# Second cross attention of a two-layer decoder kernel: VectorE spreads the queries straight from PSUM, the keys come by DMA, GpSimd copies the context values

## The chip, the cores and the metric

The kernel runs on one core of one Trainium2 chip. The metric is the device time of one execution in microseconds (us), as the median of several runs; lower is better. The core has five engines that run their own instruction streams and meet at semaphores: TensorE (PE; PEld are its weight loads), VectorE (DVE), ScalarE (ACT), GpSimd (POOL) and SyncE (SP), which here only issues DMAs.

## What is computed

The program is two decoder layers over 128 sequences of 64 tokens with 128 features, so 8192 tokens, handled as 64 tiles of 128 tokens (two sequences each). The change touches one sub-layer, the second layer's cross attention. Its heads attend to a context of the same shape, without any projection of queries, keys or values: the normalised `x` is the query, the context is key and value, the scores are bounded by a tanh, and one output projection follows.

```python
def _L1_xattn_ref(query, key, value, mask, W_out, scale, log_C):
    B, S, E, H = (4, 256, 128, 16)
    ...
    u = jnp.einsum('hbqd,hbkd->hbqk', q, k) * scale / np.sqrt(d_k)
    logits = jnp.tanh(u) * jnp.exp(log_C)
    logits = jnp.where(mask, -jnp.inf, logits)
    attn = jax.nn.softmax(logits, axis=-1)
    out_heads = jnp.einsum('hbqk,hbkd->hbqd', attn, v)
    out = jnp.moveaxis(out_heads, 0, -2).reshape(query.shape)
    return out @ W_out.T
...
x = x + _L1_xattn_ref(_layernorm(x, axis=-1), ctx_1024, ctx_1024, mask_Bx1xS2_bk0, L1_xattn_W_out, L1_xattn_scale, L1_xattn_log_C)
```

## The kernel before

The kernel goes through ten stages one after the other (attention, output norm, cross attention, memory layer, then the second layer's attention, cross attention, routing and experts). Each stage is one software pipeline per engine, written by `staggered(nc, eng, tiles, segments)`. A segment is a pair of a lag and a function; in round s an engine works through its list in the order written and calls each function for tile s minus its lag. The engines execute in order, so an instruction that waits for a semaphore holds up all that stands behind it on its engine. `need(eng, sem, T.before(n))` and `wait_ge(sem, T.now())` are the waits; `before(2)` stands where a buffer has two copies, `before(1)` where it has one.

The stage of the change is called cross1. Per tile it does this:

- DVE `normed_rows` (line 1332) writes the normalised rows to `xn`, in SBUF.
- PE `place_q` (L1102) transposes them into the PSUM tile `psXQ`, which has one copy.
- DVE `copy_queries` (L1644) copies `psXQ` to `queries`, in SBUF.
- POOL `spread_queries` (L547) multiplies `queries` by the 0/1 constant `own_head` and writes the eight-fold wider `wide_queries`, 128x1024, in which every head has its own rows only.
- DVE `copy_ctx_keys` (L1648) copies 128 columns of the transposed context, which lies in SBUF as `cT` since the start, to `ctx_keys`. The matmul takes its weights from there.
- PE `scoresT` (L899) makes the transposed scores in `psST` (one copy). It waits for the keys (`qb_ready`), the spread queries (`kx_ready`), and the tanh of the tile before.
- ACT `tanhs` (L748) and `bounded_exps` (L752) make the probabilities in `PT`.
- SP loads a tile of the context by rows to `ctile` (L445), and DVE `ctx_values` (L1636) copies it in two halves of 64 partitions to the value block `VB`, between columns of ones.
- PE `values_of_heads` (L940) multiplies probabilities and values to `psOh`; DVE `normalised_heads` divides (L1659, L1662); PE `outputT` (L954) transposes, ACT `copy_oT` (L623) copies, PE `out_project` (L970) projects to `psXY`, DVE `add_output` (L1397) adds to `x`, and `stats_of_sum` (L1653) takes the row statistics.

The order on each engine is set by hand in the lists. The semaphores `aT_raw` and `aT_ready` say that `psXQ` is written and that it may be written again, `sT_done` that a tile's scores are done, `vb_ready` that its values are in place.

Of the kernel before, what the change touches and what calls it, by code (L numbers as in the profile page):

```python
# [7 lines left out]
P = 128  # L8
SEQ = 64
HEADS = 16  # L10
DH = P // HEADS
PAIRS = HEADS // 2
SETS = 2
PER_SET = HEADS // SETS
# [21 lines left out]
ALU = mybir.AluOpType  # L36
# [71 lines left out]
def build(nc, x, ctxT, ctx, mask, consts, rows, cols, wq0, wk0, wv0, wo0, xWq, xWk, xWvT, xWeT, wqk, keysT, key_inT,  # L108
          key_out, wq1, wk1, wv1, wo1, wout, scal, router, up, down, out):
    NT = x.shape[0] // P  # L110
    NG = NT // GROUP
    with ExitStack() as es:
# [3 lines left out]
        def sem(name):  # L116
            return es.enter_context(nc.semaphore(name))
# [9 lines left out]
        small = sb("small_w", [P, 8, P])  # L127
# [19 lines left out]
        def C(name):  # L147
            a, n = CONST[name]
            return cst[:, a:a + n]
# [40 lines left out]
        queries = KC.rearrange("p u g k -> p u (g k)")  # L190
# [155 lines left out]
        ctx_in = [sem("ctx_tile0_in"), sem("ctx_tile1_in")]  # L346
        ones_ready, sums_done, quantised, folds_done, folds_ready, bound_ready = (
# [15 lines left out]

        o_seen, xT_seen, sim_seen, ln_seen, y_seen, pe_seen = sem("o_seen"), sem("xT_seen"), sem("sim_seen"), sem("ln_seen"), sem("y_seen"), sem("pe_seen")
# [43 lines left out]
        def _(sp):  # L408
# [32 lines left out]
            ctx_v = ctx.rearrange("(t p) d -> t p d", p=P)  # L441
# [4 lines left out]
            staggered(nc, sp, NT, [(0, ctx_load)])  # L446
# [21 lines left out]
        def _(pool):  # L468
# [74 lines left out]
            def spread_queries(T):  # L543

                pool.wait_ge(aT_ready, T.now(NORM["cross1"]))
                need(pool, sT_done, T.before(2))
                pool.tensor_tensor(wide_queries[:, T.u], queries[:, T.u].unsqueeze(1).to_broadcast([P, PER_SET, P]),  # L547
                                   C("own_head").unsqueeze(2).to_broadcast([P, PER_SET, P]), ALU.mult).then_inc(kx_ready, 1)
            staggered(nc, pool, NT, [(0, spread_queries)])


# [12 lines left out]
        def _(act):  # L564
# [190 lines left out]
            staggered(nc, act, NT, [(4, copy_oT(OUTT["cross1"])), (2, tanhs), (2, bounded_exps)])  # L755
# [51 lines left out]
        def _(pe):  # L807
# [80 lines left out]
            def scoresT(base):  # L888

                def seg(T):  # L890
                    u = T.u
                    pe.wait_ge(qb_ready, T.now(base))
                    pe.wait_ge(kx_ready, T.now(base))
# [204 lines left out]
            def place_q(T):  # L1098
# [5 lines left out]
                (3, values_of_heads(b2)), (4, out_project(oT_ready, OUTT["cross1"], PROJ["cross1"], lambda u: OT[:, u, :], small[:, WOUT, :])),  # L1104
# [81 lines left out]
        def _(dve):  # L1186
# [442 lines left out]
            def ctx_values(T):  # L1629

                u = T.u
                dve.wait_ge(ctx_in[u], T.pair * 16 + 16)
                need(dve, pv_done, T.before(2, b2))
                for b in range(2):
                    part = slice(SEQ * b, SEQ * b + SEQ)
                    ins = dve.tensor_copy(VBh[part, u, :, b, 0:DH], ctile[part, u, :].rearrange("p (h d) -> p h d", h=HEADS))  # L1636
                ins.then_inc(vb_ready, 1)

            def copy_queries(T):

                u = T.u
                dve.wait_ge(aT_raw, T.now(NORM["cross1"]))
                need(dve, kx_ready, T.before(2, b2))
                dve.tensor_copy(queries[:, u, :], psXQ).then_inc(aT_ready, 1)  # L1644

            def copy_ctx_keys(T):
                need(dve, sT_done, T.before(2))
                dve.tensor_copy(ctx_keys[:, T.u, :], cTt[:, T.t, :]).then_inc(qb_ready, 1)  # L1648
# [6 lines left out]
            def normalised_heads(T):  # L1655
# [8 lines left out]
            staggered(nc, dve, NT, [(1, copy_queries), (3, ctx_values), (5, add_output("cross1", None)), (0, copy_ctx_keys),  # L1664
                                    (0, normed_rows(NORM["cross1"])), (5, stats_of_sum), (3, normalised_heads)])
# [190 lines left out]
```

## Time and profile before

| | us |
|---|---|
| median of 3 runs | 2909.44 (2908.89 to 2909.66) |
| the profiled execution, its device time | 2916.36 |
| its span from the first to the last instruction | 2914.3 |
| stage cross1, from 1856.95 to 2139.72 in the span | 282.8 |

Over the span PE is busy for 2524.5 us, DVE for 2382.4, ACT for 1835.6 and POOL for 1101.8. These are averages over stages with different limits, so the table says little on cross1 alone; the rows below are from that stage wherever their group says so. The stage runs 64 tiles.

### The profile page before, as it was taken

How to read it: one execution, taken by the hardware profiler on the slowest of the kernel's cores; microseconds unless marked ns; L12 is line 12 of the kernel's file. 1: busy time of each engine (PE TensorE's matmuls, PEld its weight loads, DVE VectorE, ACT ScalarE, POOL GpSimd, SP SyncE). 2: the span in 40 equal slices, each digit the busy share in tenths (PEclk: the TensorE clock that was granted, in tenths of full speed). 3: DMA queues.
4: the chain of work that ended last, by engine and by line, in shares of the span. 5: the costliest groups of instructions: out<-in, count | busy, mean ns of one | idle time of the engine just before them, and what ended most of it. 6: DMA issues, size and time to landing. Idle time of an engine off the chain costs nothing.

```text
span 2914.3 us, 95817 instructions
## 1 busy us (share of the span) xinstructions
PE 2524.5 (87%) x35786; PEld 1958.3 (67%) x35786; DVE 2382.4 (82%) x6431; ACT 1835.6 (63%) x3307; POOL 1101.8 (38%) x981
## 2 busy tenths in 40 slices
PE   2999963867888888888799999877789999999999
PEld 2666642546777777777566666555577888888887
DVE  6999989687899999999599999677767777777776
ACT  1777763544566666666366666565666777777776
POOL 1444420008899999999323232344413000000000
PEclk9999985977999999999799999798969999999999
DMA  5000000000000000000100000000001111111111
GB/s 165 1 0 0 0 15 0 1 0 2 1 0 0 0 0 0 0 0 0 59 1 0 0 0 0 9 15 16 14 5 52 51 55 51 54 51 54 55 53 48
DMA packets 47578, 60.44 MB, mean 21 GB/s; under 512 B 6672, under 2 KB 25872, under 8 KB 47376
## 3 DMA queue, kind: packets, MB, share of 16 engines
q1 hardware_dynamic: 47504, 59.45, 6.7%
q8 instruction: 47, 0.77, 0.1%
q14 instruction: 27, 0.22, 0.0%
HBM read 54.98 MB, written 4.46 MB: 20 GB/s over the span
## 4 chain that ended last, share of the span: by engine, by line
PE 77%; DVE 13%; issue 6%; DVEq 2%; ACT 1%; POOL 1%; DMA 0%; ACTq 0%; POOLq 0%; SPq 0%
PE ps L1064 8%; PE ps L885 8%; PE ps L1053 5%; PE ps L912 4%; PE ps L927 4%; PE ps L1078 4%; PE ps L1155 4%; PE ps L1133 4%; PE ps L1157 4%; PE ps L1156 4%; PE ps L1135 4%; PE ps L1134 4%; DVE work L1587 3%; DVE work L1636 2%; PE ps L940 2%
## 5 line engine op out<-in xcount | busy, mean ns | idle before, releaser
L479 POOL TENSOR_TENSOR work<-work,consts_sb 128x1024 f32<-128x1024 f32 x128 | 243.4, 1902 | 564.9 <-ACT work L603 564.9
L1064 PEld LDWEIGHTS ps<-work 32*32 32x32 f32 x16384 | 244.0, 145 | 126.7 <-issue 125.2
L1064 PE MATMUL ps<-work 32*32 32x32 f32 x16384 | 250.2, 226 | 76.0 <-DVE work L1587 60.8
L723 ACT ACTIVATE ps<-work 128x128 f32<-128x128 f32 x512 | 154.6, 354 | 233.6 <-DVE work L1569 222.6
L885 PE MATMUL ps<-work 128*128 128x512 f32 x512 | 262.5, 615 | 4.0 <-issue 2.8
L1730 DVE TENSOR_TENSOR h_low<-consts_sb,h_up 128x1024 fp32r<-128x1024 f32 x128 | 158.3, 1237 | 110.9 <-ACT h_up L794 110.8
L1133 PE MATMUL ps<-a_low,w_up 128*128 128x512 f32 x512 | 203.0, 396 | 0.9 <-DVE a_low L1705 0.9
L1155 PE MATMUL ps<-h_low,d_up 128*128 128x512 f32 x512 | 199.6, 390 | 2.3 <-DVE h_low L1730 2.3
L1730 DVE TENSOR_TENSOR h_low<-small_w,h_up 128x1024 fp32r<-128x1024 f32 x128 | 158.8, 1240 | 51.7 <-ACT h_up L794 51.7
L1135 PE MATMUL ps<-a_up,w_low 128*128 128x512 f32 x512 | 200.2, 391 | 0.0
L1134 PE MATMUL ps<-a_up,w_up 128*128 128x512 f32 x512 | 200.0, 391 | 0.0
L1157 PE MATMUL ps<-h_up,d_low 128*128 128x512 f32 x512 | 199.3, 389 | 0.0
L1156 PE MATMUL ps<-h_up,d_up 128*128 128x512 f32 x512 | 199.2, 389 | 0.0
L547 POOL TENSOR_TENSOR work<-work,consts_sb 128x1024 f32<-128x1024 f32 x64 | 123.8, 1935 | 168.9 <-DVE work L1644 168.9
L1356 DVE TENSOR_REDUCE work<-ps 128x8 f32<-128x512 f32 x256 | 163.9, 679 | 19.8 <-PE ps L885 19.7
L594 ACT ACTIVATE work<-ps 128x512 f32<-128x512 f32 x256 | 152.6, 597 | 34.8 <-PE ps L912 31.4
L794 ACT ACTIVATE h_up<-small_w 128x1024 fp32r<-128x1024 f32 x128 | 135.8, 1061 | 50.2 <-PE ps L1157 50.2
L794 ACT ACTIVATE h_up<-consts_sb 128x1024 fp32r<-128x1024 f32 x128 | 135.8, 1061 | 48.9 <-PE ps L1157 48.8
L1053 PE MATMUL ps<-big,work 128*128 (+1 forms) x1024 | 156.8, 316 | 8.6 <-issue 3.2
L1366 DVE TENSOR_TENSOR work<-ps,work 128x512 f32<-128x512 f32 x256 | 163.4, 679 | 0.0
L912 PE MATMUL ps<-consts_sb,work 128*128 128x128 f32 x1024 | 160.5, 280 | 1.5 <-ACT work L586 1.5
L534 POOL TENSOR_SCALAR work<-work 128x512 f32<-128x512 f32 x64 | 156.4, 2444 | 12.5 <-POOL work L530 12.5
(262 smaller groups left out, 6782.5 us busy)
## 6 DMA issues: line engine op xcount, KB each, us to landing
gates_spread<-gate_rows SPq DMA_DIRECT2D x128, 256.0 KB, 3.1
ctxT_all<-in_ctxT SPq DMA_DIRECT2D x1, 4096.0 KB, 12.9
work<-in_ctx SPq DMA_DIRECT2D x64, 64.0 KB, 1.8
out<-x_all SPq DMA_DIRECT2D x16, 256.0 KB, 3.5
big<-in_up SPq DMA_DIRECT2D x1, 2048.0 KB, 8.4
consts_sb<-in_consts SPq DMA_DIRECT2D x1, 936.0 KB
w<-in_key_inT SPq DMA_DIRECT2D x1, 512.0 KB, 3.4
w<-in_key_out SPq DMA_DIRECT2D x4, 128.0 KB, 3.8
```

The source lines that it names most:

```text
L794: act.activation(h_up[:, n], hid[n], ACT.Copy).then_inc(h_up_ready, 1)
L885: pe.matmul(ps[:, g, :], QB[:, u, g, :], KX[:, u, g, :], start=not causal, stop=True).then_inc(s_done, 1)
L912: ins = pe.transpose(psPT[:, half, n * P:n * P + P], PQ[:, T.u, i * P:i * P + P], ident)
L1053: ins = pe.matmul(psH[:, c, :], KI[:, c * P:c * P + P], xTt[:, T.t, :], start=True, stop=True)
L1064: ins = pe.matmul(psW[rows, n // 16, :, n % 16], XT[rows, T.u, :, n], YT[rows, T.u, :, n], start=True, stop=True)
L1133: pe.matmul(to, upper, a_low[:, u, :], start=True, stop=False)
L1134: pe.matmul(to, upper, a_up[:, u, :], start=False, stop=False)
L1135: ins = pe.matmul(to, lower, a_up[:, u, :], start=False, stop=True)
L1155: pe.matmul(psD[e % 2], d_up[:, e, at, :], h_low[:, k % RING, c, :], start=first and c == 0, stop=False)
L1156: pe.matmul(psD[e % 2], d_up[:, e, at, :], h_up[:, k % RING, c, :], start=False, stop=False)
L1157: ins = pe.matmul(psD[e % 2], d_low[:, e, at, :], h_up[:, k % RING, c, :], start=False, stop=last and c == 1)
L1730: dve.tensor_tensor(h_low[:, n], hid[n], h_up[:, n].bitcast(F32), ALU.subtract).then_inc(h_split, 1)
```

## The change

In cross1, DVE now multiplies `psXQ` itself by `own_head` and writes `wide_queries` (128x1024) in one instruction; the copy to `queries` and the GpSimd multiplication are gone. The keys of a tile come by a DMA of their own from the transposed context in HBM, 64 KB, and the DVE copy of them is gone. The two copies of the context values go from DVE to GpSimd. The lists of four engines change. On PE, `out_project` goes ahead of `values_of_heads` and has lag 5. On ACT, the tanh goes ahead of `copy_oT`.

```diff
@@ SP
+            def keys_load(T):
+                need(sp, sT_done, T.before(2))
+                sp.dma_start(ctx_keys[:, T.u, :], ctxT_v[T.t]).then_inc(keys_in[T.u], 16)
-            staggered(nc, sp, NT, [(0, ctx_load)])
+            staggered(nc, sp, NT, [(0, ctx_load), (0, keys_load)])
@@ POOL
-            def spread_queries(T):
-                pool.wait_ge(aT_ready, T.now(NORM["cross1"]))
-                need(pool, sT_done, T.before(2))
-                pool.tensor_tensor(wide_queries[:, T.u], queries[:, T.u].unsqueeze(1).to_broadcast([P, PER_SET, P]),
-                                   C("own_head").unsqueeze(2).to_broadcast([P, PER_SET, P]), ALU.mult).then_inc(kx_ready, 1)
+            def ctx_values(T):
+                u = T.u
+                pool.wait_ge(ctx_in[u], T.pair * 16 + 16)
+                need(pool, pv_done, T.before(2, ATTN["cross1"]))
+                pool.sem_inc(ctx_seen, 1)
+                for b in range(2):
+                    part = slice(SEQ * b, SEQ * b + SEQ)
+                    ins = pool.tensor_copy(VBh[part, u, :, b, 0:DH], ctile[part, u, :].rearrange("p (h d) -> p h d", h=HEADS))
+                ins.then_inc(vb_ready, 1)
@@ ACT
-            staggered(nc, act, NT, [(4, copy_oT(OUTT["cross1"])), (2, tanhs), (2, bounded_exps)])
+            staggered(nc, act, NT, [(2, tanhs), (4, copy_oT(OUTT["cross1"])), (2, bounded_exps)])
@@ PE, scoresT
-                    pe.wait_ge(qb_ready, T.now(base))
-                    pe.wait_ge(kx_ready, T.now(base))
+                    pe.wait_ge(keys_in[u], T.pair * 16 + 16)
+                    pe.wait_ge(aT_ready, T.now(NORM["cross1"]))
@@ PE
-                (3, values_of_heads(b2)), (4, out_project(oT_ready, OUTT["cross1"], PROJ["cross1"], lambda u: OT[:, u, :], small[:, WOUT, :])),
+                (5, out_project(oT_ready, OUTT["cross1"], PROJ["cross1"], lambda u: OT[:, u, :], small[:, WOUT, :])), (3, values_of_heads(b2)),
                 (0, place_q), (1, scoresT(b2)), (3, outputT(b2, n2))])
@@ DVE
-            def ctx_values(T):
...
-            def copy_queries(T):
...
-            def copy_ctx_keys(T):
...
+            def spread_queries(T):
                 dve.wait_ge(aT_raw, T.now(NORM["cross1"]))
                 need(dve, sT_done, T.before(2))
+                dve.tensor_tensor(wide_queries[:, T.u], psXQ.unsqueeze(1).to_broadcast([P, PER_SET, P]), own_head, ALU.mult)\
+                    .then_inc(aT_ready, 1)
-            staggered(nc, dve, NT, [(1, copy_queries), (3, ctx_values), (5, add_output("cross1", None)), (0, copy_ctx_keys),
-                                    (0, normed_rows(NORM["cross1"])), (5, stats_of_sum), (3, normalised_heads)])
+            staggered(nc, dve, NT, [(0, normed_rows(NORM["cross1"])), (1, spread_queries), (5, add_output("cross1", None)), (5, stats_of_sum), (3, normalised_heads)])
```

What stands in a row on DVE in one round of cross1 (the last one written out ahead of the loop), before the change:

```order
L1644 COPY work<-ps 128x128
L1636 COPY work<-work 64x16x8 x2
L1397 TENSOR_TENSOR x_all<-ps,x_all 128x128
L1648 COPY work<-ctxT_all 128x128
L1332 TENSOR_SCALAR work<-x_all,mv,rstd 128x128
L1653 BN_STATS st_all<-x_all 128x6
L1659 RECIPROCAL work<-ps 128x16
L1662 TENSOR_TENSOR work<-ps,work 128x8x2x8
```

The same round on DVE after the change, with the new file's line numbers (L1341 is `normed_rows`, L1644 the spreading, L1406 `add_output`, L1650 the statistics, L1656 and L1659 the division):

```order
L1341 TENSOR_SCALAR work<-x_all,mv,rstd 128x128
L1644 TENSOR_TENSOR work<-ps,consts_sb 128x1024
L1406 TENSOR_TENSOR x_all<-ps,x_all 128x128
L1650 BN_STATS st_all<-x_all 128x6
L1656 RECIPROCAL work<-ps 128x16
L1659 TENSOR_TENSOR work<-ps,work 128x8x2x8
```

Nine instructions became six: the copy of the queries, the two copies of the values and the copy of the keys went, and one of 128x1024 came.

One round of PE before the change, from the last rounds ahead of its loop (L940 values, L970 output projection, L1102 `place_q`, L899 scores, L954 `outputT`):

```order
L940 MATMUL ps<-work 64x18 x16
L970 MATMUL ps<-small_w,work 128x128
L1102 MATMUL ps<-consts_sb,work 128x128
L899 MATMUL ps<-work 64x512 x4
L954 MATMUL ps<-consts_sb,work 64x64 x4
```

The same round of PE after it, with the new line numbers (L979 output projection, L949 values, L1111 `place_q`, L908 scores, L963 `outputT`):

```order
L979 MATMUL ps<-small_w,work 128x128
L949 MATMUL ps<-work 64x18 x16
L1111 MATMUL ps<-consts_sb,work 128x128
L908 MATMUL ps<-work 64x512 x4
L963 MATMUL ps<-consts_sb,work 64x64 x4
```

Only the projection moved, ahead of the values and to a tile that is one older; PE has the same instructions as before.

## Rows read from the trace of the kernel before

**Rows 1.** Stretches: us, busy us (instructions) of each engine, PEclk, DMA share, GB/s.

```profile
1500.00:1600.00 100.00, 98.41 (x1161) 65.59 (x1159) 91.10 (x192) 66.93 (x172) 28.88 (x16) 1.00 0.00 0
1858.00:2131.00 273.00, 212.99 (x3165) 141.06 (x3166) 204.61 (x558) 159.87 (x188) 123.79 (x64) 0.87 0.05 15
2003.00:2005.00 2.00, 2.00 (x13) 0.71 (x14) 0.98 (x5) 0.00 (x0) 1.28 (x1) 0.50 0.00 0
1873.00:1881.00 8.00, 8.00 (x81) 5.32 (x81) 3.94 (x14) 3.93 (x5) 2.51 (x2) 0.50 0.07 18
```

**Rows 2.** Timeline of cross1, two tiles: start us, us, engine, line, count.

```profile
1993.10 1.11 PE L940 MATMUL ps<-work 128*64 128x18 f32 x32 [1.74 <-DVE work L1636]
...
1995.92 1.11 PE L940 MATMUL ps<-work 128*64 128x18 f32 x32
...
1998.82 2.13 DVE L1636 COPY work<-work 64x128 f32<-64x128 f32 x2
...
1998.97 1.89 POOL L547 TENSOR_TENSOR work<-work,consts_sb 128x1024 f32<-128x1024 f32 x1 [1.68 <-DVE work L1644]
...
2001.20 1.11 PE L940 MATMUL ps<-work 128*64 128x18 f32 x32 [1.89 <-DVE work L1636]
...
2005.42 1.26 PE L940 MATMUL ps<-work 128*64 128x18 f32 x32
...
2018.31 1.11 PE L940 MATMUL ps<-work 128*64 128x18 f32 x32 [1.89 <-DVE work L1636]
```

**Rows 3.** Lines of cross1, by engine: busy us, mean ns, idle us before, releasers.

```profile
L1662 DVE TENSOR_TENSOR work<-ps,work 128x128 f32<-128x128 f32 x64 | 18.6, 291 | 7.2
...
L1659 DVE RECIPROCAL work<-ps 128x16 f32<-128x16 f32 x64 | 16.1, 252 | 27.7 <-PE ps L940 27.5
...
L623 ACT ACTIVATE work<-ps 128x128 f32<-128x128 f32 x64 | 17.7, 277 | 103.6 <-PE ps L954 103.6
...
L940 PE MATMUL ps<-work 128*64 128x18 f32 x2048 | 76.1, 218 | 52.4 <-DVE work L1636 50.5 <-issue 1.5 <-ACT work L752 0.4
```

**Rows 4.** Single lines, all their executions: duration ns min/median/max, first to last start.

```profile
L1644 DVE COPY work<-ps x64: 280/291/293, 1858.0 to 2127.0; 128x128 f32<-128x128 f32 x64
...
L1636 DVE COPY work<-work x128: 209/226/1921, 1863.9 to 2134.1; 64x128 f32<-64x128 f32 x128
...
L1332 DVE TENSOR_SCALAR work<-x_all,mv,rstd x128: 332/344/2045, 1437.0 to 2125.5; 128x128 f32 x112, 128x128 f32<-128x128 f32 x16
...
L1397 DVE TENSOR_TENSOR x_all<-ps,x_all x64: 290/292/293, 1875.7 to 2139.0; 128x128 f32 x56, 128x128 f32<-128x128 f32 x8
...
L1653 DVE BATCH_NORM_STATS2 st_all<-x_all x64: 277/284/295, 1877.6 to 2139.4; - x56, 128x6 f32<-128x128 f32 x8
...
L1599 DVE TENSOR_TENSOR work<-ps,work x64: 1185/1210/1224, 683.8 to 1427.5; 128x1024 f32<-128x1024 f32 x64
```

**Rows 5.** Timeline of the start of cross1: start us, us, engine, line.

```profile
1863.92 1.11 ACT L748 ACTIVATE work<-ps,scalars 128x1024 f32<-128x1024 f32 x1
...
1865.07 1.24 ACT L752 ACTIVATE work<-work,mbias,scalars 128x1024 f32<-128x1024 f32 x1
...
1865.29 1.98 PE L899 MATMUL ps<-work 64*64 64x512 f32 x8 [1.68 <-ACT work L748]
...
1867.33 1.11 ACT L748 ACTIVATE work<-ps,scalars 128x1024 f32<-128x1024 f32 x1 [1.02 <-PE ps L899]
...
1884.34 1.09 PE L899 MATMUL ps<-work 64*64 64x512 f32 x8
```

**Rows 6.** POOL lines elsewhere in the program, their executions: ns min/median/max.

```profile
L499 POOL TENSOR_TENSOR work<-work x64: 402/413/432, 657.1 to 1394.9; 128x128 f32<-128x128 f32 x64
...
L534 POOL TENSOR_SCALAR work<-work x64: 2362/2450/2510, 664.4 to 1402.4; 128x512 f32<-128x512 f32 x64
```

**Rows 7.** SP's DMA of the context rows in cross1: issue ns, and landing.

```profile
L445 SPq DMA_DIRECT2D work<-in_ctx x64: 332/333/423, 1856.9 to 2129.5; - x64
...
DMA to landing us min/median/max: 1.7/1.8/3.2
```

More of the change, by code:

```diff
@@ L189, in build @@
         ctx_keys = work[:, q_at:q_at + 2 * P].rearrange("p (u c) -> p u c", u=2)
-        queries = KC.rearrange("p u g k -> p u (g k)")
         wide_queries = work[:, top[0] - 2 * HEADS * SEQ:top[0] - 2 * HEADS * SEQ + 2 * PER_SET * P].rearrange("p (u j c) -> p u j c", u=2, j=PER_SET)
@@ L346, in build @@
         ctx_in = [sem("ctx_tile0_in"), sem("ctx_tile1_in")]
+        keys_in = [sem("ctx_keys0_in"), sem("ctx_keys1_in")]
         ones_ready, sums_done, quantised, folds_done, folds_ready, bound_ready = (
@@ L362, in build @@
         ln_step, ln_ready, squares_done = sem("ln_step"), sem("ln_ready"), sem("squares_done")
+        ctx_seen = sem("ctx_seen")
         o_seen, xT_seen, sim_seen, ln_seen, y_seen, pe_seen = sem("o_seen"), sem("xT_seen"), sem("sim_seen"), sem("ln_seen"), sem("y_seen"), sem("pe_seen")
@@ L440, in _ @@
             sp.wait_ge(phase, PHASE["cross1"])
-            ctx_v = ctx.rearrange("(t p) d -> t p d", p=P)
+            ctx_v, ctxT_v = ctx.rearrange("(t p) d -> t p d", p=P), ctxT.rearrange("p (t c) -> t p c", c=P)
             def ctx_load(T):
@@ L541, in _ @@
             pool.wait_ge(phase, PHASE["cross1"])
-            def spread_queries(T):
-                pool.wait_ge(aT_ready, T.now(NORM["cross1"]))
-                need(pool, sT_done, T.before(2))
-                pool.tensor_tensor(wide_queries[:, T.u], queries[:, T.u].unsqueeze(1).to_broadcast([P, PER_SET, P]),
-                                   C("own_head").unsqueeze(2).to_broadcast([P, PER_SET, P]), ALU.mult).then_inc(kx_ready, 1)
-            staggered(nc, pool, NT, [(0, spread_queries)])
+            def ctx_values(T):
[7 more added lines that the diff above has]
+                ins.then_inc(vb_ready, 1)
+            staggered(nc, pool, NT, [(0, ctx_values)])
             def lower_weights(e):
@@ L1627, in _ @@
             b2 = ATTN["cross1"]
-            def ctx_values(T):
[L1631 to L1637, printed above, removed]
-            def copy_queries(T):
-                u = T.u
+            own_head = C("own_head").unsqueeze(2).to_broadcast([P, PER_SET, P])
+            def spread_queries(T):
                 dve.wait_ge(aT_raw, T.now(NORM["cross1"]))
-                need(dve, kx_ready, T.before(2, b2))
-                dve.tensor_copy(queries[:, u, :], psXQ).then_inc(aT_ready, 1)
-            def copy_ctx_keys(T):
                 need(dve, sT_done, T.before(2))
-                dve.tensor_copy(ctx_keys[:, T.u, :], cTt[:, T.t, :]).then_inc(qb_ready, 1)
+                dve.tensor_tensor(wide_queries[:, T.u], psXQ.unsqueeze(1).to_broadcast([P, PER_SET, P]), own_head, ALU.mult)\
+                    .then_inc(aT_ready, 1)
             def stats_of_sum(T):
```

## The prediction

> **What bounds the kernel now.** The change touches one stage, so I first asked where that stage's time goes. Three stretches compared [rows 1]: in the attention stage before, PE is busy for 98.4 of 100 us at full clock (1.00); in cross1 for 213.0 of 273 us, with a mean clock of 0.87, while DVE is busy for 204.6. So in cross1 nobody is full. The timeline [rows 2] shows why. The values of successive tiles (L940) start at 1993.10, 1995.92, then only at 2001.20, 2005.42, and four tiles later the pattern is back: 2001.20 to 2018.31 is 17.11 us, or 4.28 a tile. Over the whole stage the query copy L1644 gives the same, 1858.0 to 2127.0 for 63 steps, 4.27 a tile [rows 4].
>
> The first distance, 2.82 us, is a tile in which PE went through its whole round at full clock without a stop. That is what PE needs. The rest is waiting, and the lines of the stage name the wait: PE sat idle for 52.4 us ahead of L940, 50.5 of them for DVE's copy of the values, L1636 [rows 3]. One such wait can be followed. The two copies begin at 1998.82 and take 2.13 us, POOL's spreading begins at 1998.97 and takes 1.89 us, and PE starts L940 at 2001.20, just behind [rows 2]. A copy of 64x128 takes 209 ns at least, 226 in the median and 1921 at most [rows 4]: the maximum is the length of POOL's instruction. So a DVE copy between SBUF places stops when POOL is running, and DVE's in-order queue, the values, and PE stop with it. ACT's `copy_oT` meanwhile waits 103.6 us for `outputT` (L954), and the tanh stands behind it [rows 3].
>
> The Trainium skill, "SBUF — State Buffer", section "Who interferes with whom", gives a reason: VectorE and GpSimd share one pair of SBUF ports as an exclusive lock, which a copy of the two-port kind takes, and an instruction with at most one SBUF input outside these modes does not. By this rule the trace agrees: L1644 reads PSUM and never leaves 280 to 293 ns.
>
> **The change, part by part**, per tile.
>
> *Removed on DVE:* the copy of the queries, 0.29 us, two of the values at 0.63 in the mean (80.5 us over 128 would be 0.21 each without the stops, 0.42 a tile), and the copy of the keys, at least the 0.21 of a copy of half its partitions [rows 4].
>
> *Added on DVE:* one 128x1024 multiplication from PSUM. The same shape, also with PSUM and SBUF inputs, takes 1.21 us (L1599) [rows 4]. The new DVE round is 0.34 (L1332) + 1.21 + 0.29 (L1397) + 0.28 (L1653) [rows 4] + 0.25 (L1659) + 0.29 (L1662) [rows 3] = 2.66 us. That fits under PE's 2.82, but with only 0.16 to spare.
>
> *POOL:* the 1.9 us instruction is replaced by two copies of 64x128. No such copy stands in the trace. The nearest row has the same length and also eight-element rows, 0.41 us for 128x128 with two inputs (L499); a badly strided one, 2.45 us for 512 elements (L534), gives 0.61 for 128 [rows 6]. At 0.2 from below (DVE's own 0.21), the bounds are 0.4 and 1.22 us a tile; I take 0.83, by the row that it is most like. The values are issued once the tile two before is through `values_of_heads`, so nearly two tiles, 5.6 us, hide DMA and copies. The cover would be gone at some 3.5 us of copies.
>
> *SP:* one more DMA a tile. The 64 KB of context rows take 0.33 us to issue and land after 1.8 us in the median, 3.2 at most [rows 7]. The keys are fetched from rows that lie far apart, which no DMA of this size here shows; I bound it by 1.8 and, twice the worst, 6.4. The keys of tile t are asked for when the scores of tile t-2 are done, so two tiles must hold L899 (1.09 [rows 5]), 0.33, and the landing: 1.09 + 0.33 + 3.2 = 4.6 us against 5.64. SP works through context rows and keys alternately; the context's wait (for POOL's copies two tiles back) ends at about the same point, so I cost this at nothing up to a landing of 4.2 us.
>
> *ACT:* the tanh no longer stands behind `copy_oT`, which waits for PE's last instruction of the round. ACT's own work is 1.11 + 1.24 [rows 5] + 0.28 [rows 3] = 2.63 us. The loop over the single `psST` is scores 1.09, 0.06 from the scores' end to the tanh (1867.27 to 1867.33), tanh 1.11, and 0.26 from its end (1865.03) to the next scores at 1865.29 [rows 5]: 2.52 us. So neither sets the tile.
>
> *PE:* the same instructions. The projection moves ahead of the values and takes a tile that is one older, so it fills time in which probabilities may be late; cost nothing, gain inside the 2.82. The wait for `normed_rows` at `place_q` also shrinks, since that is now DVE's first instruction of a round.
>
> *What is late next:* `place_q` waits until DVE has spread the tile before. From the values' end DVE has 0.25 + 0.29 (division) + 0.34 + 1.21 = 2.09 us until the spread is there, and then 0.57 for `add_output` and statistics. PE needs the spread one round on. It closes, barely. The same section of the Trainium skill speaks against the change as well: `normed_rows` is a tensor_scalar from SBUF to SBUF, which by it can take the shared pair. The trace agrees: the median of L1332 is 344 ns, its maximum 2045 [rows 4]. Now it can only meet copies of 0.41 us in place of 1.9, so when it does the DVE round is 3.07 us.
>
> *The sum.* PE's floor is 2.82 us; 2% of idle as in the attention stage [rows 1] makes it 2.88; an occasional stop of L1332 brings me to 2.95. With PE never idle for 2 us, the clock should stay at 1.00 as in that stage [rows 1], instead of falling to 0.50 in one tile in four. The stage starts at half clock, though (0.50 while PE is 8.00 of 8 us busy [rows 1]): the scores at 1865.29 and 1884.34 are four tiles apart, 4.76 a tile [rows 5], and the new order can't make this faster. Five tiles at 4.76 instead of 2.95 are 9 us; if the denser work brings the clock back earlier, fewer; I take 7. Before: 63 x 4.27 = 269.0, and the stage is 282.8, so filling, draining and moments take 13.8. After: 63 x 2.95 = 185.9, + 13.8 + 7 = 206.7 us. Saved: 76.1. The profiled execution's 2916.4 would become 2840.3. It lies 7 us above the median of the runs, 2909.4, which becomes **2833 us**. No other stage changes: the GpSimd, SP and ACT work behind cross1 starts when it ends.
>
> **The rivals.**
>
> *A, the forecast* (0.62): PE sets the tile, 2.82 to 3.1 us. At 2.82 with only 3 us of start loss: 177.7 + 16.8 = 194.5, time 2821. At 3.1: 195.3 + 20.8 = 216.1, time 2843.
>
> *B, a hop remains on the path* (0.20): DVE's 2.66 us and its stops leave too little slack, and `place_q` or the scores wait for the spread in each round. The other distance between values that a short wait gives in today's rounds is about 3.3 us (half a microsecond over 2.82). 63 x 3.3 = 207.9, + 20.8 = 228.7, time 2855. For it speaks that three engines are within 0.2 us of each other, against it that rounds overlap by two buffers everywhere but at `psXQ`, `psST` and `psOh`.
>
> *C, the clock keeps falling* (0.12): one tile in four like that at 2001.20, 4.22 us [rows 2], gives a mean of (3 x 2.95 + 4.22) / 4 = 3.27, and 63 x 3.27 + 20.8 = 226.8, time 2853. For it: most of this stage's matmuls are tiny, 18 columns. Against it: the clock fell after stretches without any matmul, and these should go.
>
> *D, slower: the keys' DMA* (0.03). If the landing took L, two tiles last 1.09 + 0.33 + L. It equals today's 8.54 us at L = 7.1 and the kernel is slower above that; at 8 the tile is 4.71 us, and the time 2909.4 - 282.8 + 63 x 4.71 + 20.8 = 2944. Against it stands the worst landing of 3.2 us for the same number of bytes, on queues with a share of 0.05 [rows 1].
>
> *E, the stops merely move* (0.03): the change would not do what it says, as `normed_rows` stops for both copies in each round at the slowest GpSimd price. 2.66 + 1.22 = 3.88 us a tile, 63 x 3.88 + 20.8 = 265.2, time 2892.
>
> **Range and chances.** A to C hold 0.94 between 2821 and 2855; the edges for a spread landing or start loss beyond these put me at 2818 to 2860. Faster by over 0.2% (5.8 us, about what a measurement of this kernel can tell from no change) are A, B, C and two thirds of E: 0.96. Within 0.2% is the last third of E, with the copies dearer still: 0.01. Slower: 0.03, D.
>
> **What the profile would show.** Right: in cross1 L940 starts every 2.9 us with no DVE line named as its releaser, PE busy for over 90% and PEclk near 1.00 after the first 25 us; DVE's spreading at 1.21 us and DVE about 90% busy; POOL's copies at 0.4 us each; the keys landing near 2 us, never awaited. Wrong if: `place_q` or the scores wait for the spread in each round (B), PEclk stays under 0.9 (C), a DMA is the releaser of L899's successor (D), or L1332's successor has a mean far over 0.35 us (E). The likeliest error is the half-clock start, worth up to 9 us, and the 0.16 us between DVE and PE.

## The result, and the profile after

| | before | after |
|---|---|---|
| median of 4 runs | 2909.55 (2908.89 to 2916.86) | 2844.94 (2837.63 to 2846.59) |
| the profiled execution, its device time | 2916.36 | 2846.45 |
| its span | 2914.3 | 2844.7 |
| cross1 in the span | 282.8 | 215.6 (1854.17 to 2069.75) |

The ratio of the runs on record, after to before, is 0.9768, with a 95% interval of 0.9748 to 0.9788 (that of the two medians alone is 0.9778): faster. Of the 69.6 us by which the spans differ, 67.2 lie in cross1; the stage also began 2.8 us earlier, and what follows it gave 0.4 back.

The stretches of the changed kernel: us, then the busy us and instructions of PE, PEld, DVE, ACT and POOL, PEclk, DMA share, GB/s. The first is the whole stage less its ends, the second lies in its start, the third is the steady part.

```profile
1858.00:2060.00 202.00, 197.87 (x3138) 135.14 (x3136) 152.48 (x365) 156.20 (x186) 36.41 (x122) 0.92 0.14 40
...
1866.00:1889.00 23.00, 23.00 (x220) 14.61 (x216) 11.03 (x25) 10.44 (x14) 2.61 (x9) 0.50 0.10 27
...
1900.00:2050.00 150.00, 148.35 (x2516) 102.88 (x2515) 122.73 (x298) 122.71 (x148) 29.80 (x100) 1.00 0.15 43
```

Beside [rows 1], PE is busy for 198 of 202 us in place of 213 of 273. In the steady part it is busy for 148.35 of 150 us at full clock; the mean of 0.92 comes from the start alone.

The lines of the stage (busy us, mean ns, idle us before, releasers), against [rows 3] and [rows 4]:

```profile
L949 PE MATMUL ps<-work 128*64 128x18 f32 x2048 | 75.5, 217 | 0.0
...
L1644 DVE TENSOR_TENSOR work<-ps,consts_sb 128x1024 f32<-128x1024 f32 x63 | 76.7, 1218 | 1.2 <-PE ps L1111 1.2
...
L1341 DVE TENSOR_SCALAR work<-x_all,mv,rstd 128x128 f32 x56 | 19.4, 346 | 7.3 <-issue 7.3
...
L1659 DVE TENSOR_TENSOR work<-ps,work 128x128 f32<-128x128 f32 x64 | 18.7, 292 | 7.2
...
L1650 DVE BATCH_NORM_STATS2 st_all<-x_all x56 | 16.5, 294 | 13.9 <-DVE x_all L1406 13.9
...
L632 ACT ACTIVATE work<-ps 128x128 f32<-128x128 f32 x64 | 17.3, 270 | 2.9 <-PE ps L963 2.9
```

The values, which waited 52.4 us before, wait 0.0 now. The spreading is never stopped (mean 1218 ns), nor is `normed_rows` (346). `copy_oT` waits 2.9 us in place of 103.6.

The instructions that moved, all executions (ns min/median/max, first to last start), and the keys' landing:

```profile
L556 POOL COPY work<-work x128: 288/298/407, 1856.0 to 2061.1; 64x128 f32<-64x128 f32 x128
...
L450 SPq DMA_DIRECT2D work<-in_ctxT x64: 332/333/432, 1854.5 to 2056.3; - x64
...
DMA to landing us min/median/max: 1.7/1.8/2.2
```

What waits in the stage now, the longest sums: who, for whom, us in all, times, longest.

```profile
POOL work L556 <- PE ps L949: 164.0, 62, 7.7
ACT work L757 <- PE ps L908: 45.1, 63, 3.0
PEld ps L963 <- issue: 38.5, 69, 0.8
DVE st_all L1650 <- DVE x_all L1406: 14.6, 61, 0.3
DVE work L1656 <- PE ps L949: 12.2, 9, 5.0
DVE x_all L1406 <- PE ps L979: 9.7, 8, 1.5
DVE work L1341 <- issue: 7.3, 27, 0.3
```

POOL and ACT have time to spare. PE's own waits stand further down and come to 4.5 us in four times, none of them in 1900 to 2050. DVE waits for PE only at the start (9 and 8 times), but in nearly every tile (61 times, 0.24 us each) for its own sum before it can take the statistics. In 1900 to 2050 DVE is busy for 122.73 us, and its idle time is 12.1 us ahead of the statistics, 6.7 at the turn of the loop (L1341), 6.2 ahead of the product (L1659) and 2.4 ahead of the reciprocal (L1656). That is 150.1 of 150 us, and the profile names no other engine as the cause of any of it.

The timeline of a tile and a bit (start us, us, engine, line, count):

```profile
1962.51 1.11 PE L949 MATMUL ps<-work 128*64 128x18 f32 x32
...
1964.58 1.22 DVE L1644 TENSOR_TENSOR work<-ps,consts_sb 128x1024 f32<-128x1024 f32 x1
...
1965.48 1.11 PE L949 MATMUL ps<-work 128*64 128x18 f32 x32
...
1966.26 0.29 DVE L1650 BATCH_NORM_STATS2 st_all<-x_all  x1 [0.24 <-DVE x_all L1406]
...
1967.59 0.35 DVE L1341 TENSOR_SCALAR work<-x_all,mv,rstd 128x128 f32 x1 [0.27 <-issue]
...
1967.85 1.22 DVE L1644 TENSOR_TENSOR work<-ps,consts_sb 128x1024 f32<-128x1024 f32 x1
...
1968.57 1.11 PE L949 MATMUL ps<-work 128*64 128x18 f32 x32
```

The values are 2.97 and 3.09 us apart, where the unhindered round in [rows 2] took 2.82. The spreadings are 3.27 apart here and 2.80 in the next tile, as the loop holds two tiles and pays its turn (0.27) once; in the mean a tile takes 3.04 us (44 tiles between 1905 and 2040).

### The profile page after: what moved, and what is told of

Read it like the earlier page. It is cut to its first block, busy times and chain, and to the rows that moved or that the text cites. A ratio compares the mean times of both kernels' runs of the same rounds, so it can differ in the third digit from the quotient of the medians.

```text
span 2844.7 us, 95835 instructions
## 1 busy us (share of the span) xinstructions
PE 2507.1 (88%) x35786; PEld 1949.9 (69%) x35786; DVE 2333.9 (82%) x6239; ACT 1834.5 (64%) x3307; POOL 1016.5 (36%) x1045
## 4 chain that ended last, share of the span: by engine, by line
PE 81%; DVE 10%; issue 5%; DVEq 1%; ACT 1%; POOL 1%; DMA 0%; ACTq 0%; POOLq 0%; SPq 0%
PE ps L1073 9%; PE ps L894 8%; PE ps L1062 5%; PE ps L921 5%; PE ps L936 4%; PE ps L1087 4%; PE ps L1164 4%; PE ps L1166 4%; PE ps L1142 4%; PE ps L1165 4%; PE ps L1144 4%; PE ps L1143 4%; DVE work L1596 3%; PE ps L908 3%; PE ps L949 2%
## 5 line engine op out<-in xcount | busy, mean ns | idle before, releaser
L484 POOL TENSOR_TENSOR work<-work,consts_sb 128x1024 f32<-128x1024 f32 x128 | 243.6, 1903 | 563.1 <-ACT work L612 563.1
L589 ACT ACTIVATE work<-ps 128x128 f32<-128x128 f32 x128 | 35.5, 278 | 194.9 <-PE ps L845 194.9
```

## The experiments

Each is told against the kernel before on the same chip: its median (2911.22 us in the first set of four, 2911.91 in the second, 2912.5 in the third), the ratio with its 95% interval, and the steady tile, which is the distance of the spreadings at full clock, taken from some 40 tiles of the profile. Edits are shown against the changed kernel unless it is said otherwise. The first set asks what the new orders and the start are worth, the second takes the work apart, the third follows the two questions that these left.

**The changed kernel again**, for the spread of its own time.

> The changed kernel itself, beside the variants of this call, so that they can be compared on one chip. Expected 2838 to 2847 us, as its earlier runs; 3.03 us a tile in cross1 once the clock is full.

2840.02 us (2835.27 to 2844.2), 0.9765 [0.9749, 0.9782], tile 3.04. Its profiled span is 2833.5 us, 11.2 less than the first profile's, with the same steady tile. The first spreading begins at 1847.4 in place of 1855.1, so 7.7 us of this were there before the stage began. The spreadings take 198.5 us from the first to the last in place of 203.3: that is the other part, and it lies in the start. What follows gives 1.2 back. The clock was full from about 1872 on, some 24 us behind the first spreading, and in the first profile only from about 1890 on, 35 us behind it. The profiles of the other kernels begin the stage between 1850 and 1859 as well, although nothing ahead of it was changed in most of them. A difference of some microseconds between two profiles can therefore be put down to an edit only if it is seen inside the stage.

**The PE list as before.**

> PE's list back to values, projection of the tile four back, place_q, scores, outputT; all else as in the changed kernel. Theory A: PE is the limit, and its new order costs it 0.15 us a tile (3.03 against the 2.82 of an unhindered tile before), so this comes to 2.82 to 2.9 us a tile and is 8 to 13 us faster than the changed kernel (2832 to 2837). Theory B: the new order is needed because the projection fills time in which the probabilities are late; then PE waits ahead of the values and this is slower, 3.2 us a tile or more, 2855 and up.

```diff
-                (5, out_project(oT_ready, ...)), (3, values_of_heads(b2)),
+                (3, values_of_heads(b2)), (4, out_project(oT_ready, ...)),
```

2848.37 us, 0.9795 [0.9778, 0.9812], tile 3.24. This is neither theory as it stood: it is slower, as theory B has it, but the wait is not ahead of the values, and 2855 isn't reached. In 1900 to 2050 this wait is new:

```profile
PE ps L979 <- ACT work L632: 12.8, 47, 0.3
```

With lag 4 the projection waits 0.27 us in each of the 47 rounds for a `copy_oT` that was released at the end of the round before. The new PE list is worth 0.20 us a tile, 8 us between the medians; the two intervals just touch, but no run of the one is as fast as any of the other.

**The ACT list as before.**

> ACT's list back to copy of the output first, then tanh, exp; all else as in the changed kernel. Theory A: PE is the limit and ACT has 0.4 us of slack a tile, so this changes nothing beyond 3 us. Theory B: the tanh behind the copy, which waits for PE's last instruction of a round, closes a loop through psST: outputT's end 0.53, copy 0.17, tanh 1.11, then scores and outputT again 0.26 + 1.3, about 3.4 us a tile, and 20 to 25 us slower than the changed kernel.

```diff
-            staggered(nc, act, NT, [(2, tanhs), (4, copy_oT(OUTT["cross1"])), (2, bounded_exps)])
+            staggered(nc, act, NT, [(4, copy_oT(OUTT["cross1"])), (2, tanhs), (2, bounded_exps)])
```

2843.12 us, 0.9769 [0.9753, 0.9785], tile 3.04, 3.1 us above the changed kernel, so theory A. The tanh ahead of `copy_oT` is worth nothing that shows.

**A warm start: six matmuls ahead of the stage** into PSUM banks that nothing uses then; nobody reads them.

> The changed kernel with six extra 128x512 matmuls on PE ahead of cross1, into PSUM banks that the stage does not use, in the 5.8 us in which PE waits for the row moments. Theory A: this gap is why the stage runs its first 35 us at half clock; filled, the stage starts at full clock and the time falls by up to (4.8 - 3.03) us x 7 tiles = 12 us, to about 2833. Theory B: the half clock comes from what the first rounds themselves are like (few columns, waits), so the clock still falls within some us and the time is that of the changed kernel, within 3 us.

```diff
             b2 = ATTN["cross1"]
+            for n in range(6):
+                pe.matmul(ps[:, 2 + n % 2, :], ident, cT[:, 0:512], start=True, stop=True)
```

2839.96 us, 0.976 [0.9742, 0.9778]: no gain over the changed kernel in the medians. The clock was full when the stage began and fell all the same, as theory B has it. Its stretches, and the two waits of PE at that place in its timeline:

```profile
1854.00:1858.00 4.00, 2.59 (x14) 0.87 (x12) 2.61 (x5) 0.00 (x0) 1.18 (x4) 1.00 0.27 78
1858.00:1860.00 2.00, 0.80 (x9) 0.14 (x1) 1.77 (x3) 1.39 (x2) 0.00 (x0) 0.77 0.13 37
1860.00:1872.00 12.00, 10.74 (x104) 6.08 (x106) 4.32 (x9) 7.00 (x7) 1.18 (x4) 0.50 0.10 30
```

```profile
1857.18 0.30 PE L1113 MATMUL ps<-consts_sb,work 128*128 128x128 f32 x1 [1.41 <-DVE work L1646]
...
1861.26 1.98 PE L908 MATMUL ps<-work 64*64 64x512 f32 x8 [2.07 <-ACT work L757]
```

PE is idle for 1.41 us in the second round, ahead of `place_q`, and for 2.07 in the third, ahead of the scores; the matmul at 1861.26 already takes 1.98 us in place of 1.09. The 0.77 of the two microseconds up to 1860 is the mean of 1.00 and 0.50, so the clock fell at about 1859.1: behind the gap of 1.41 us, and before the one of 2.07 had begun (1859.19). The extra matmuls stood ahead of the wrong gaps. In this profile the spreadings take 194.7 us from the first to the last, 4 to 9 less than in the two of the changed kernel; that the medians don't show it stays open.

**The values back on DVE**, POOL without work in the stage; the keys still come by DMA.

> The two copies of the context values back on DVE (lag 2, behind the spreading), GpSimd has nothing to do in cross1; keys by DMA, all orders as in the changed kernel. Theory 'stops' (what cost the time before was a DVE copy that waited for GpSimd's 1.9 us instruction): the copies now take 0.21 us each, DVE comes to 2.66 + 0.42 = 3.08 us a tile, and the time is within 10 us of the changed kernel. Theory 'load' (DVE simply had too much to do): DVE at 3.1 us sets the tile and with its waits for its own results (0.5 us) it is 3.6, 35 us slower than the changed kernel.

```diff
+            def ctx_values(T):
...
+                    ins = dve.tensor_copy(VBh[part, u, :, b, 0:DH], ctile[part, u, :].rearrange("p (h d) -> p h d", h=HEADS))
-            staggered(nc, dve, NT, [(0, normed_rows(...)), (1, spread_queries), (5, add_output("cross1", None)), ...])
+            staggered(nc, dve, NT, [(0, normed_rows(...)), (1, spread_queries), (2, ctx_values), (5, add_output("cross1", None)), ...])
```

2866.5 us, 0.9848 [0.9831, 0.9866], tile 3.40: 26 us more than the changed kernel, so between the two theories and nearer to 'load'. DVE's time in the changed kernel was full, and 0.44 us of copies, at 220 ns each, cost 0.36 us a tile.

**The keys back on DVE**, first in its round; POOL still copies the values.

> The keys by a DVE copy of 128x128 again, first in the round, in place of the DMA; values stay on GpSimd. The copy is between SBUF places, so it can stop for one of GpSimd's copies of 0.3 us. Theory A: PE is the limit, DVE's 2.66 + 0.22 stays under it: within 5 us of the changed kernel. Theory B: DVE's slack is used up by its waits for its own results, so 0.22 us a tile shows, 14 us slower.

```diff
-            staggered(nc, sp, NT, [(0, ctx_load), (0, keys_load)])
+            staggered(nc, sp, NT, [(0, ctx_load)])
+            def copy_ctx_keys(T):
+                need(dve, sT_done, T.before(2))
+                dve.tensor_copy(ctx_keys[:, T.u, :], cTt[:, T.t, :]).then_inc(qb_ready, 1)
-            staggered(nc, dve, NT, [(0, normed_rows(...)), ...])
+            staggered(nc, dve, NT, [(0, copy_ctx_keys), (0, normed_rows(...)), ...])
```

2861.39 us, 0.983 [0.9813, 0.9847], tile 3.40, 21 us more than the changed kernel: theory B, and more than its 14 us. Here 0.23 us of work cost 0.36, since the copy also waits for the scores in 1900 to 2050:

```profile
DVE work L1638 <- PE ps L904: 17.9, 44, 0.4
```

**Both back on DVE**: it spreads and copies values and keys, POOL is idle, and the PE and ACT lists are those of before. The edit is shown against the kernel before.

> Only the spreading moved: DVE spreads from PSUM, and also copies values and keys; GpSimd idle; PE's and ACT's lists as in the kernel before. Theory 'stops': DVE has 2.66 + 0.42 + 0.22 = 3.3 us of work with no stops, the tile is 3.4 to 3.6 us, and more than half of the gain is kept: 2865 to 2880. Theory 'load': DVE has more to do than in the kernel before (3.3 against 2.6 us without the stops), so the tile is as long as before or longer, 2905 us and up.

```diff
@@ POOL
-            def spread_queries(T):
...
@@ DVE
-            staggered(nc, dve, NT, [(1, copy_queries), (3, ctx_values), (5, add_output("cross1", None)), (0, copy_ctx_keys),
-                                    (0, normed_rows(...)), (5, stats_of_sum), (3, normalised_heads)])
+            staggered(nc, dve, NT, [(0, copy_ctx_keys), (0, normed_rows(...)), (1, spread_queries), (2, ctx_values),
+                                    (5, add_output("cross1", None)), (5, stats_of_sum), (3, normalised_heads)])
```

2959.06 us, 1.0169 [1.0147, 1.0192]: slower than before, though POOL runs nothing that could stop DVE's copies now. The number is one that theory 'load' allowed; the reason turned out to be another. The timeline shows a ring (keys' copy L1637, sum L1391, projection L964, scores L893):

```profile
1964.61 1.09 PE L893 MATMUL ps<-work 64*64 64x512 f32 x8
...
1965.88 0.23 DVE L1637 COPY work<-ctxT_all 128x128 f32 x1 [0.74 <-PE ps L893]
...
1966.38 1.22 DVE L1643 TENSOR_TENSOR work<-ps,consts_sb 128x1024 f32<-128x1024 f32 x1
1967.51 0.46 DVE L1632 COPY work<-work 64x128 f32<-64x128 f32 x2
1968.00 0.29 DVE L1391 TENSOR_TENSOR x_all<-ps,x_all 128x128 f32 x1
1968.34 0.49 PE L964 MATMUL ps<-small_w,work 128*128 128x128 f32 x2 [1.23 <-DVE x_all L1391]
```

The scores release the copy at DVE's head; behind it stand rows, spread, values and sum; the sum frees the one `psXY` for the next projection, and behind that stand `place_q` and the next scores. PE's and DVE's work follow one another instead of overlapping: PE idles 1.23 us at the projection, DVE 0.74 at the keys. And the clock goes with it, 0.66 in the mean:

```profile
1900.00:2100.00 200.00, 170.66 (x1997) 111.99 (x1997) 119.68 (x353) 98.61 (x119) 0.00 (x0) 0.66 0.04 13
```

**The new lists of PE and ACT alone**, on the kernel before, which the edit is shown against.

> The kernel before with only the new orders on PE and ACT. Theory 'stops': PE still waits for the stopped copies of the values, so the gain is small, 0 to 10 us. Rival: the tanh behind the copy of the output was what held the rounds together, and the orders alone give 25 us or more.

```diff
-            staggered(nc, act, NT, [(4, copy_oT(OUTT["cross1"])), (2, tanhs), (2, bounded_exps)])
+            staggered(nc, act, NT, [(2, tanhs), (4, copy_oT(OUTT["cross1"])), (2, bounded_exps)])
-                (3, values_of_heads(b2)), (4, out_project(oT_ready, ...)),
+                (5, out_project(oT_ready, ...)), (3, values_of_heads(b2)),
```

2916.75 us, 1.0024 [1.0007, 1.0042]; the spreadings are 4.37 us apart over the whole stage, against 4.27 in the kernel before. Without the rest they bring nothing, and cost some 5 us: DVE's sum (L1397) now waits 45.6 us for the later projection (L970) between 1858 and 2120, in 37 rounds.

**Copies that cannot stop**, on the kernel before: DVE's copies of values and keys become multiplications by ones that lie in PSUM. The data, the order and POOL's spreading stay. The edit, shown against the kernel before, changes two things at once, the operation (a copy becomes a tensor_tensor) and the place of one operand.

> The kernel before, with one thing changed: DVE's copies of the values and of the keys are multiplications by ones that stand in PSUM, so that they read PSUM and only one SBUF operand, as the copy of the queries does, which never stopped. DVE has slightly more work (0.29 us in place of 0.21), GpSimd still runs its 1.9 us instruction in each tile. Theory 'stops': PE no longer waits for the values, and the tile falls from 4.27 to 3.0 to 3.4 us: 2830 to 2856, most of the gain of the change without it. Theory 'load' (DVE's work and the order of the lists hold the tile at 4.27): 2905 or more.

```diff
+            ones_ps = bank(2, 0)
+            dve.tensor_copy(ones_ps, ones[:, :])
-                    ins = dve.tensor_copy(VBh[...], ctile[...])
+                    ins = dve.tensor_tensor(VBh[...], ones_ps[part]..., ctile[...], ALU.mult)
-                dve.tensor_copy(ctx_keys[:, T.u, :], cTt[:, T.t, :]).then_inc(qb_ready, 1)
+                dve.tensor_tensor(ctx_keys[:, T.u, :], ones_ps, cTt[:, T.t, :], ALU.mult).then_inc(qb_ready, 1)
```

2852.34 us (2843.42 to 2855.29), 0.9792 [0.9765, 0.9818], tile 3.22: 60 us of gain with the old division of work, inside the range of theory 'stops'. The value copy over all its executions (ns min/median/max), and the lines of 1900 to 2050:

```profile
L1638 DVE TENSOR_TENSOR work<-ps,work x128: 272/290/297, 1863.0 to 2067.4; 64x128 f32<-64x128 f32 x128
```

```profile
L547 POOL TENSOR_TENSOR work<-work,consts_sb 128x1024 f32<-128x1024 f32 x47 | 89.1, 1896 | 62.2 <-DVE work L1647 62.2
...
L1332 DVE TENSOR_SCALAR work<-x_all,mv,rstd 128x128 f32 x46 | 49.0, 1065 | 0.0
L940 PE MATMUL ps<-work 128*64 128x18 f32 x1473 | 51.4, 212 | 6.1 <-DVE work L1638 6.1
```

The copy never exceeds 297 ns, where it stood up to 1921 in [rows 4], although POOL's instruction still takes 1.9 us. Instead `normed_rows`, which was left in its old form, meets POOL in each tile and takes 1065 ns in the mean. The Trainium skill's "SBUF — State Buffer", section "Who interferes with whom", says that a DVE instruction with at most one SBUF input, outside the two-port modes, does not contend with GpSimd, and that copy and tensor_scalar can enter these modes. The trace agrees on both: 297 ns at most for the one kind, 1065 in the mean for the other. Which of the two changes is needed, the operation or the operand, was not taken apart.

The run also says why the stops before were so dear. In the kernel before they added 1.2 us a tile: 0.84 for two copies of the values (0.63 for 0.21 each) and 0.35 for that of the keys (0.58 in the mean for 0.23). Here they add 0.72 (1065 less 346 ns), so 0.5 less, but the tile is 1.05 us shorter. Before, DVE was idle for 1.07 us a tile as well (204.6 busy of 273 us), 51 of those 68 us waiting for PE, which had waited 50.5 us for DVE's values; and the clock was 0.87 in the mean. Here DVE is busy for 135.97 of 150 us and waits for no other engine in that time. By these rows a stop at this place only makes DVE's round longer; ahead of the values it made PE wait too, and then DVE for PE.

**Both back on DVE, with the new lists**, and the keys' copy behind the spreading: the ring of the POOL-idle run opened. The edit is shown against that run.

> As the variant with GpSimd idle (DVE spreads, copies values and keys), but with the new lists of PE and ACT, and with the copy of the keys behind the spreading. In the first such variant, with the old lists, a ring closed in each round: scores, copy of the keys, rows, spreading, values, add_output, projection, scores: 4.2 us at full clock. Theory: the new lag of the projection opens the ring, so that only DVE's load is left, and each of the two offloads is worth 0.35 us a tile as measured alone: 3.75 us a tile, 2882 to 2890. Rival: without both offloads the ring closes all the same, 4.2 us a tile, 2910 and up.

```diff
-            staggered(nc, dve, NT, [(0, copy_ctx_keys), (0, normed_rows(...)), (1, spread_queries), (2, ctx_values), ...])
+            staggered(nc, dve, NT, [(0, normed_rows(...)), (1, spread_queries), (0, copy_ctx_keys), (2, ctx_values), ...])
```

(and the PE and ACT lists of the changed kernel.) 2864.26 us, 0.9834 [0.9813, 0.9855], tile 3.53, 18 us below the range of its theory. So the ring, and the half clock that came with it, not DVE's work, made that run slow: 95 us come back with the same instructions, and the clock is at 1.00 from 1900 to 2050. PE's list, ACT's list and the place of the keys' copy changed together; which of them opens the ring is not shown. Against 3.04, the two offloads together are worth 0.50 us a tile, and not 0.36 + 0.36: the keys' copy waits for the scores at the head of DVE's round, and behind the spreading it does not.

**Values first, with lag 5 for the projection**, and on DVE the division ahead of the sum: to give PE its 2.82 us round back.

> The changed kernel with the projection of the tile five back, as in the change, but behind the values on PE, as in the kernel before; on DVE the division goes ahead of add_output and its statistics, so that add_output does not wait for the later projection. Theory A: PE is the limit and is never idle; its round got longer by its order alone (0.41 us from the projection to the next instruction behind outputT, against 0.33 behind the values; place_q 0.26 behind the values against 0.20 behind the projection). Then a tile falls from 3.04 to about 2.88 us, 10 us in all: 2828 to 2836. Theory B: DVE's chain sets the round at 3.04 and PE only fills it; then this is within 3 us of the changed kernel or slower.

```diff
-                (5, out_project(oT_ready, ...)), (3, values_of_heads(b2)),
+                (3, values_of_heads(b2)), (5, out_project(oT_ready, ...)),
-            staggered(nc, dve, NT, [..., (1, spread_queries), (5, add_output("cross1", None)), (5, stats_of_sum), (3, normalised_heads)])
+            staggered(nc, dve, NT, [..., (1, spread_queries), (3, normalised_heads), (5, add_output("cross1", None)), (5, stats_of_sum)])
```

2837.91 us (2827.4 to 2843.63), 0.9741 [0.9717, 0.9766], tile 3.06: theory B. PE's timeline:

```profile
1961.73 1.11 PE L949 MATMUL ps<-work 128*64 128x18 f32 x32
...
1964.55 1.11 PE L949 MATMUL ps<-work 128*64 128x18 f32 x32
...
1966.13 0.14 PEld L1111 LDWEIGHTS ps<-consts_sb,work 128*128 128x128 f32 x1 [0.24 <-DVE work L1644]
...
1967.84 1.11 PE L949 MATMUL ps<-work 128*64 128x18 f32 x32
```

PE does one tile in 2.82 us, and in the next waits for the spreading, 3.29. Its busy time fell to 145.72 of 150 us, the tile did not. DVE's did not change either: busy for 122.87 us, and idle for 27.3 behind its own results and the loop's turn, together 150. So what sets 3.05 is DVE and not PE.

**That order, and nine matmuls to fill PE's first gaps**: the six ahead of the stage, one ahead of the second `place_q`, two ahead of the second scores. The edit is shown against the values-first run.

> The variant with values first and lag 5, and besides nine extra 128x512 matmuls into unused PSUM banks: six ahead of the stage, one ahead of the second place_q, two ahead of the second scores, in the gaps after which the clock fell in the variant with six alone. Theory A: the half-clock start comes from these gaps: the stage stays at 1.00 and saves 5 to 7 tiles x 1.8 us, so 2818 to 2828. Theory B: the few columns of the first rounds let the clock fall in any case, and this equals the variant without the extra matmuls within 3 us.

```diff
+            for n in range(6):
+                pe.matmul(ps[:, 2 + n % 2, :], ident, cT[:, 0:512], start=True, stop=True)
@@ PE, place_q
+                if isinstance(T.t, int) and T.t == 1:
+                    pe.matmul(ps[:, 2, :], ident, cT[:, 0:512], start=True, stop=True)
@@ PE, scoresT
+                    if isinstance(T.t, int) and T.t == 1:
+                        for n in range(2):
+                            pe.matmul(ps[:, 2 + n, :], ident, cT[:, 0:512], start=True, stop=True)
```

2833.24 us (2827.4 to 2834.99), 0.9727 [0.9708, 0.9746], tile 3.05. Its first stretches:

```profile
1851.00:1856.00 5.00, 4.45 (x18) 1.55 (x16) 3.47 (x8) 0.00 (x0) 1.18 (x4) 1.00 0.22 64
1856.00:1861.00 5.00, 4.26 (x46) 1.82 (x43) 2.05 (x3) 4.40 (x4) 0.00 (x0) 1.00 0.10 29
1861.00:1866.00 5.00, 4.93 (x96) 3.42 (x94) 3.87 (x8) 4.68 (x6) 1.18 (x4) 1.00 0.16 43
```

The clock stays at 1.00, as theory A has it, but the time lies between its 2828 and what theory B gives. The twelve distances from the first spreading to the thirteenth come to 35.1 us, against 40.3 with the six matmuls alone, 45.6 in the order without extra matmuls and 44.0 in the changed kernel's second profile. This is the fastest of all kernels here, by 6.8 us below the changed kernel's second median and 11.7 below its first. Its interval lies just clear of both of the changed kernel's; against the same order without the extra matmuls the intervals overlap, and there only the profile's start shows the gain.

## Why the prediction was right

**The bound of before and its cause: right, and shown.** The ones-in-PSUM run takes away the stops of the value and key copies, and 60 of 65 to 71 us come (64.6 in the first comparison, 71.2 in the second), though each of these copies is longer than one that isn't stopped (0.29 us for 0.23). The rest fits the new PE list (0.20 us a tile), which brought nothing by itself on the old kernel; that the two add up to the whole was not run.

**Who sets the tile: wrong, inside a range that was wide enough.** Forecast A says that PE sets the tile. The values-first run, in which PE can do 2.82 us and the tile stays, shows that it is DVE. The step that failed is the comparison of 2.66 us for DVE with 2.82 for PE, 0.16 to spare. This is the weakness that rival B named, and that the prediction's last lines name as one of its two likeliest errors, though B's sign, a wait for the spread in each round, did not come. The range of 2818 to 2860 holds the numbers of A, B and C alike, so the hit alone doesn't tell them apart; 2844.94 lies even just above the 2843 of A's upper end.

**The tile: 2.95 forecast, 3.04 measured.** This term was mis-sized. DVE's durations overlap a little, so that it is busy for only 122.73 us in 150, 2.49 a tile. But its waits for its own results were not in the sum: 0.24 for the sum ahead of the statistics, 0.12 for the reciprocal ahead of the product (6.2 us in 1900 to 2050), 0.05 ahead of the reciprocal, 0.13 for the turn of the loop (0.27 in each second tile). That is 3.03, the tile but for rounding. PE's round in the new order is 3.04 as well, without a gap; whether it could be shorter in this order is not shown.

**The new PE list: "cost nothing, gain inside the 2.82".** It gains 0.20 us a tile, by a wait that the prediction did not name, that of the projection for `copy_oT`. Without it the kernel would have had a tile of 3.24, near rival B's 3.3 but by another hop than B's.

**The start: 7 us forecast, 11.7 measured.** In the profiled run five tiles, between the spreadings at 1866.21 and 1891.69, take 5.10 us each; (5.10 - 3.04) x 5 = 10.3. The steady tiles at half clock came out dearer than [rows 5] gave (4.76). The three distances ahead of them, with the first rounds, give the rest.

**The sum.** From the first spreading to the last it is 203.3 us, 63 x 3.04 = 191.5 and 11.7 for the start. Filling and draining take 12.3, where the forecast took over the 13.8 of before. Together these are the measured 215.6 against 206.7: 5.6 more by the tile, 4.7 by the start, 1.5 less by the filling. The stage began 2.8 us earlier, which the forecast had not, so the profiled execution is 2846.45 in place of 2840.3. The other half of the miss is that the profile of after lies only 1.5 us above its median and not 7 like that of before: 6.1 + 5.5 are the 12 us between 2833 and 2845, but for the rounding.

**DVE's share**: about 90% busy was forecast, and it is 82% (122.73 of 150 us); what was missing in the sum is idle time, not work. **The keys' copy** had stops too: 0.58 us in the mean before, where the prediction removed "at least" 0.21. **The buffers**: the prediction says that rounds overlap by two buffers everywhere but at `psXQ`, `psST` and `psOh`. `psXY` has one copy as well, and the ring of the POOL-idle run closes through it. **POOL's copy**: 0.30 us (0.41 was the row taken). **The keys**: landing 1.8 us, 2.2 at most, and PE never waits for them. **The ACT list**: nothing in the steady state, as its round of 2.5 to 2.6 us is covered. **`normed_rows`**: mean 346 ns, so even the occasional stop that the forecast allowed for did not come; without the 0.07 us that it allowed for them the forecast would have been 2.88, 0.16 below the measured tile. That 2.95 came within 0.09 is in part luck.

**The rivals.** The clock that keeps falling did not come: 1.00 over the whole of 1900 to 2050. Neither did the slow landing. That the stops merely move is what the ones-in-PSUM run did, to 1065 ns in `normed_rows`, yet it was fast. The price of this rival, 3.88 us a tile, came from 1.22 us of stops; 0.72 came there, beside the 1.9 us instruction. That DVE's round grows by them was right, as DVE is full in that run; but PE waits for `normed_rows` only twice in its 64 tiles.

**Not settled:** whether the old division of work with copies that can't stop would reach 3.04 under the new PE list; it wasn't tried. Its DVE is busy for 135.97 of 150 us and waits for nobody, at 3.22 us a tile, which speaks against it. Nor is it known why some runs keep the half clock for two more tiles than others.

## What to carry to other kernels

When an instruction's maximum equals the length of another engine's instruction, look at what stands behind it in its queue: moving the work is one cure, and writing the copy as a multiplication with one operand in PSUM is a smaller one, which gave 60 of 65 to 71 us here. When two engines are within a few tenths of a microsecond of each other, count a round by the distance of one instruction to its next execution, not by summed durations, since waits for an engine's own results and loop turns are not in these. Before work is piled on an engine to free another, follow the ring through its single buffers: the same instructions took 2959 us with one set of lists and 2864 with another.

## What the runs showed of the hardware that was not expected

- The granted clock stays at 0.50 (the 1.2 GHz level) long after PE has no more gaps: 23 us of 23 busy in the changed kernel. In the run with six extra matmuls it fell at about 1859.1, behind PE gaps of 1.41 and 0.39 us. In the run with three more matmuls, whose gaps are 0.55, 0.39 and 0.35 us, it was 1.00 (2.4 GHz) from the first tile on. These are one profile each, and the three matmuls were not taken apart.
- POOL's copy of 64x128 in eight-element pieces takes 0.298 us in the median, 0.07 more than DVE's 0.226, and it never stops `normed_rows`, which takes 0.34 to 0.35 us throughout the stage.
- A multiplication of 64x128 with one operand in PSUM takes 0.290 us where the copy between SBUF places takes 0.226: the price of a copy that cannot be stopped is 0.064 us.
- 64 KB from rows that lie far apart land as fast as the context's rows, both 1.8 us in the median.
